# Attention with the key blocks of a step packed into nine full-width blocks of exponentials and a ring of four

## The reference

```python
# first attention: q per head, k and v shared
scores = jnp.einsum('bnhd,bmd->bhnm', q, k) / jnp.sqrt(jnp.float32(D))
scores = jnp.where(causal, -jnp.inf, scores)
out = jnp.einsum('bhnm,bmd->bnhd', jax.nn.softmax(scores, axis=-1), v)
# second attention: k and v per head
scores = jnp.einsum('bhqd,bhkd->bhqk', q, k) / scale + _alibi_bias(H, Tlen)[None]
out = jnp.einsum('bhqk,bhkd->bhqd', jax.nn.softmax(scores, axis=-1), v)
```

## Time and profile before

| | |
|---|---|
| median of three runs | 1051.63 us (1050.88 to 1053.87) |
| the profiled execution, span of its core | 1051.1 us |
| TensorE busy | 997.1 us, 95% of the span |
| VectorE busy | 759.5 us, 72% |
| ScalarE busy | 589.0 us, 56% |
| GpSimd busy | 410.8 us, 39% |
| exponentials (L1403) | 768, 329.0 us |
| values (L1055) | 1536 rows, 163.7 us |
| masks (L760) | 120, 76.2 us |

### The profile page before, as it was taken

One profiled execution on the slowest core, in us unless ns is written; L12 is line 12 of the kernel. 1 busy time (PEld: TensorE's weight loads), 2 busy tenths in 40 slices (PEclk: granted clock), 3 DMA queues, 4 the chain that ended last, 5 costly groups with the idle time before them and its releaser, 6 DMA issues.

```text
span 1051.1 us, 19787 instructions
## 1 busy us (share of the span) xinstructions
PE 997.1 (95%) x6818; PEld 638.7 (61%) x6818; DVE 759.5 (72%) x1564; ACT 589.0 (56%) x1262; POOL 410.8 (39%) x434
## 2 busy tenths in 40 slices
PE   4899999999999999999999999999999999999998
PEld 3533333433348889988886434343343588899887
DVE  6788888888547686447878888888883558764575
ACT  4525776777764335653344657677777643456432
POOL 3420544322443507725743102323234362274470
PEclk9869999999999999999999999999999999999999
DMA  4721212110114415644249533234401152256351
GB/s 133 193 41 30 47 42 43 39 43 13 28 28 149 142 46 155 188 116 118 79 112 227 107 51 57 50 72 74 76 12 44 42 201 60 73 179 165 119 180 51
DMA packets 66755, 95.23 MB, mean 91 GB/s; under 512 B 19669, under 2 KB 50821, under 8 KB 64599
## 3 DMA queue, kind: packets, MB, share of 16 engines
q1 hardware_dynamic: 46645, 52.54, 18.5%
q10 hardware_dynamic: 13100, 22.53, 8.8%
q0 software_dynamic: 6912, 18.88, 7.0%
HBM read 66.59 MB, written 26.67 MB: 89 GB/s over the span
## 4 chain that ended last, share of the span: by engine, by line
PE 74%; DVE 13%; ACT 4%; DMA 3%; issue 3%; POOL 2%; SPq 1%; ACTq 0%; DVEq 0%; POOLq 0%
PE o_ps L1055 14%; PE st_ps L1037 11%; PE su_ps L996 7%; PE st_ps L245 7%; PE st_ps L246 7%; PE st_ps L247 6%; DVE mab L1677 4%; PE st_ps L996 3%; PE o_ps L1195 3%; PE su_ps L1195 3%; PE su_ps L1101 2%; ACT pt L1403 2%; PE st_ps L1230 2%; PE su_ps L1000 2%; DVE xn L1561 1%
## 5 line engine op out<-in xcount | busy, mean ns | idle before, releaser
L1403 ACT ACTIVATE pt<-st_ps 128x512 f32<-128x512 f32 (+3 forms) x768 | 329.0, 495 | 174.4 <-PE st_ps L1037 117.4
L1037 PE MATMUL st_ps<-qs,ks 99*128 99x512 bf16 (+9 forms) x768 | 245.0, 332 | 9.6 <-ACT pt L1403 7.0
L760 POOL TENSOR_SCALAR_AFFINE_SELECT pt<-pt 128x512 f32<-128x512 f32 x120 | 76.2, 635 | 351.5 <-ACT pt L1403 351.5
L1677 DVE TENSOR_REDUCE mab<-su_ps 128x1 f32<-128x512 f32 (+3 forms) x302 | 190.0, 659 | 23.4 <-PE su_ps L1000 16.2
L996 PE MATMUL su_ps<-ks,qs 102*128 102x512 bf16 (+7 forms) x538 | 162.3, 331 | 4.7 <-DVE mc L1677 2.7
L1055 PE MATMUL o_ps<-pt,vp 128*32 128x512 f32 (+3 forms) x1536 | 163.7, 501 | 1.9 <-POOL pt L760 1.0
L1037 PEld LDWEIGHTS st_ps<-qs,ks 99*128 99x128 bf16 (+2 forms) x768 | 73.7, 98 | 116.0 <-ACT pt L1403 65.0
L841 POOL DMA_INDIRECT rows_in<-rows,source x80 | 79.0, 987 | 97.5 <-DVE source L1937 73.7
L1677 DVE TENSOR_REDUCE mab<-st_ps 128x1 f32<-128x512 f32 (+2 forms) x152 | 100.2, 660 | 13.7 <-PE st_ps L1000 10.6
L1429 ACT CAST hh<-hf 128x512 fp32r<-128x512 f32 x64 | 39.7, 621 | 124.4 <-DVE hf L1892 124.4
L996 PEld LDWEIGHTS su_ps<-ks,qs 96*128 96x128 bf16 (+1 forms) x538 | 52.8, 99 | 84.0 <-DVE mab L1677 48.5
(11 more groups left out here) (230 smaller groups left out, 2031.4 us busy)
## 6 DMA issues: line engine op xcount, KB each, us to landing
wu_raw<-w_units_dram SPq DMA_DIRECT2D x32, 384.0 KB, 3.2
outs<-rows_out ACTq DMA_DIRECT2D x40, 256.0 KB, 2.7
q_parts<-hml SPq DMA_DIRECT2D x16, 384.0 KB, 3.4
wexp_raw<-w_units_dram SPq DMA_DIRECT2D x16, 384.0 KB, 7.2
inv<-inverses SPq DMA_DIRECT2D x128, 32.0 KB, 1.8
rows<-xn SPq DMA_DIRECT2D x8, 512.0 KB, 6.6
qs<-q_parts ACTq DMA_DIRECT2D x10, 384.0 KB
k_parts<-hml SPq DMA_DIRECT2D x8, 384.0 KB, 2.5
```

Source lines behind the costliest of these rows:

```text
L760: pool.affine_select(block, block, [[0, 4], [1, P]], ALU.is_ge, 0.0, base=0, channel_multiplier=-1).then_inc(masked, 1)
L1037: last = pe.matmul(bank[KM_BANKS[n % len(KM_BANKS)]][:, lo - CH * part:hi - CH * part], key_stack(l, s)(j)[0:rows, P * kt:P * kt + P], que ...
L1403: act.activation(exponentials(s, q, lo, hi)[:, j, :], bank[KM_BANKS[i % len(KM_BANKS)]][:, lo - CH * part:hi - CH * part], ACT.Exp, scale= ...
L1677: dve.tensor_reduce(to, bank[SU_BANKS[n % len(SU_BANKS)]][:, 0:share * width].rearrange("p (j k) -> p j k", j=share), AX.X, ALU.max).then_ ...
```

## The change

The pairs (`kt`, `part`) of a step are packed into blocks of 512 columns. Six pairs are that wide by themselves; of the other six, (1,0) and (3,0), (2,0) and (6,1), (5,1) and (7,1) lie side by side in one bank. A later step has nine blocks, so 36 pieces (`LATER_BLOCKS`), the first ten, so 40 (`FIRST_BLOCKS`; there (2,0) and (6,1) stay alone, 256 wide, and the first half has three blocks). A joined block has two score matmuls a piece, one exponential, one or two masks, and the values of its two pairs one behind the other. Blocks take the four places of `pt` in turn, and an exponential waits for the values of the block four earlier. In all there are 584 exponentials for 768. GpSimd's other work is bound to masked blocks, of which there are five for eight, and stands at other places; in the last step the two halves' divisions of the step before stand behind the second and third masked block, and the reciprocal roots (`rstds`) together behind the last. `FC_BEHIND`, `PV_LAG` and the lead of the units are as before; the units are spread over the new pieces by the same rule, and `SECOND_AT` of the second layer is 7 for 9.

The diff's core:

```diff
+FIRST_BLOCKS = [((0, 0),), ((1, 0), (3, 0)), ((2, 0),),
+                ((0, 1),), ((1, 1),), ((4, 1),), ((2, 1),), ((5, 1), (7, 1)), ((6, 1),), ((3, 1),)]
+LATER_BLOCKS = [((0, 0),), ((0, 1),), ((1, 0), (3, 0)), ((4, 1),), ((2, 0), (6, 1)), ((1, 1),), ((5, 1), (7, 1)), ((2, 1),), ((3, 1),)]
+HALF_BLOCKS = 3
+FIRST_PIECES = 4 * len(FIRST_BLOCKS)
+RING_OF_BLOCKS = 4
...
-SECOND_AT = (HALF_PIECES - 1, 9)
+SECOND_AT = (HALF_PIECES - 1, 7)
...
+        def exponentials(S, q):
+
+            own, at = divmod((block_base(S) + q) % RING_OF_BLOCKS, 2)
+            return pt[:, own, :, CH * at:CH * at + CH]
...
+                    if masks_after(l, s):
+                        own = exponentials(S, q)
+                        pool.wait_ge(p_ready, piece_base(S) + 4 * q + 4)
+                        for at in diagonals(s, q):
...
+            def last_step(l, i):
+
+                if i == 0:
                     split_unit(l, 0)
-                if kt == 1:
+                if i == 1:
                     divide(l, STEPS - 2, 0)
-                if kt == 2:
+                if i == 2:
+                    divide(l, STEPS - 2, 1)
+                if i == 3:
                     split_unit(l, 1)
-                if kt == 3:
-                    divide(l, STEPS - 2, 1)
-                    rstds(2 * l + 1, 0, 1)
-                if kt == 4:
-                    rstds(2 * l + 1, 1, 2)
+                if i == 4:
+                    rstds(2 * l + 1, 0, 2)
...
+                for kt, part, lo, hi, at in spans(s, q):
+                    diagonal = lo == P * kt and not masks_after(l, s)
+                    last = pe.matmul(out_b[:, at:at + hi - lo], key_stack(l, s)(j)[0:rows, P * kt:P * kt + P],
+                                     query_columns(s, slice(0, rows), j, lo, hi), start=True, stop=not diagonal)
...
+                for i, (kt, part, lo, hi, at) in enumerate(spans(s, q)):
+                    if kt == 0:
+                        wait(pe, ou_done, 2 * S - 1 + part)
+                    for j in range(4):
...
-                        if last_quad(S, q) is not None:
-                            act.wait_ge(pv_done, last_quad(S, q) + 1)
-                        act.activation(exponentials(s, q, lo, hi)[:, j, :], bank[KM_BANKS[i % len(KM_BANKS)]][:, lo - CH * part:hi - CH * part], ACT.Exp,
+                        wait(act, pv_done, block_base(S) + q - RING_OF_BLOCKS + 1)
+                        act.activation(exponentials(S, q)[:, j, 0:width_of(s, q)], bank[KM_BANKS[i % len(KM_BANKS)]][:, 0:width_of(s, q)], ACT.Exp,
```

More of the change, by code:

```diff
@@ L142, in units_behind_pieces @@
 def units_behind_pieces(l, lead):
-    work = np.array([[queries(s, n // 4)[1] - queries(s, n // 4)[0] + P for n in range(PIECES)] for s in range(STEPS)], float)
-    at = (np.arange(STEPS)[:, None] + np.cumsum(work, 1) / work.sum(1)[:, None]).flatten()
+    work = [np.array([width_of(s, n // 4) + P for n in range(4 * len(blocks(s)))], float) for s in range(STEPS)]
+    at = np.concatenate([s + np.cumsum(w) / w.sum() for s, w in enumerate(work)])
     cost = np.array([share * width + P for _, _, _, share, width, _ in SU] + [4 * CH], float)
@@ L163, in units_behind_pieces @@
         for u, t in enumerate(s - 1 - lead + through):
-            while at[n] < t - 1e-9 or u > 1 and n < PIECES - 1:
+            while at[n] < t - 1e-9 or u > 1 and n < FIRST_PIECES - 1:
                 n += 1
@@ L1046, in values @@
                 b, g = divmod(s, G)
-                kt, part = quads(s)[q]
-                if kt == 0:
-                    wait(pe, ou_done, 2 * S - 1 + part)
-                lo, hi = queries(s, q)
-                if lo == P * kt and masks_after(l, s):
-                    pe.wait_ge(masked, QT * mask_turn(l, s) + kt + 1)
-                pe.wait_ge(p_ready, PIECES * S + 4 * q + 4)
-                for j in range(4):
-                    last = pe.matmul(o_ps[32 * j:32 * j + 32, lo:hi], vp[:, QT * b + kt, 4 * g + j if l else 4 * (g % 2), :],
-                                     exponentials(s, q, lo, hi)[:, j, :], start=kt == 0,
-                                     stop=kt == (QT if part else HALF) - 1)
+                if diagonals(s, q) and masks_after(l, s):
+                    pe.wait_ge(masked, QT * mask_turn(l, s) + sum(len(diagonals(s, n)) for n in range(q + 1)))
+                pe.wait_ge(p_ready, piece_base(S) + 4 * q + 4)
+                for i, (kt, part, lo, hi, at) in enumerate(spans(s, q)):
+                    if kt == 0:
+                        wait(pe, ou_done, 2 * S - 1 + part)
+                    for j in range(4):
+                        last = pe.matmul(o_ps[32 * j:32 * j + 32, lo:hi], vp[:, QT * b + kt, 4 * g + j if l else 4 * (g % 2), :],
+                                         exponentials(S, q)[:, j, at:at + hi - lo], start=kt == 0, stop=(q, i) == last_of(s, part))
                 last.then_inc(pv_done, 1)
@@ L1084, in attention @@
                             transpose_half(l, 1)
-                    if s == STEPS - 1 and piece in FC_BEHIND:
-                        output_projection(l, FC_BEHIND[piece])
-                for q in range(NQ - PV_LAG, NQ):
+                    if s == STEPS - 1 and 4 * q + j in FC_BEHIND:
+                        output_projection(l, FC_BEHIND[4 * q + j])
+                for q in range(len(LATER_BLOCKS) - PV_LAG, len(LATER_BLOCKS)):
                     values(l, STEPS - 1, q)
```

128 lines of the change are left out of this document (57 added, 71 removed).

## The result

The changed kernel takes 1043.54 us (median of four runs, 1042.43 to 1046.84); the kernel before took 1051.26 beside it (the three runs given ahead and one more, 1050.33 to 1053.87). The ratio is 0.9923, with a 95% interval of 0.9901 to 0.9945. 1044.8 had been forecast. The profiled execution, 1046.84 us with a span of 1045.1, is the slowest of the four, so the two spans differ by 6.0 where the medians differ by 7.7.

What follows compares the result with a forecast made beforehand. TensorE's work and waits were taken as the bound. 10.0+2.0-2.6-2.0-.6 = 6.8 us less than the median of 1051.63 gave 1044.8; forecast 1038.5 to 1048.5 (chance .60), 8-in-10 range 1037.5 to 1056.

Steps and rivals of the forecast that it cites:

- What bounds the kernel: TensorE, busy 997.1 of 1051.1 us: time can be won only where it works or waits for something.
- Joined blocks: In a later attention step, three value groups fewer on TensorE save .6 us (ends .45 and .75).
- both terms of a join: A group's fixed .15 us and the .1 for entering it from a score matmul; with both, a later step saves .75.
- the back-to-back row: Trace row of adjacent 256- and 128-column value groups at half clock: .72 us at full clock against .93 alone, saving .21.
- The first rival: Joins save nothing or waits return: a step gains .3 to .5 instead of 1.0; 1049 to 1054 us, chance .19.
- Waits: TensorE's 1.32 us of waits a steady step become .65 to 1.2; with joins, the step gains 1.0, ten steps 10.0.
- The maxima: Their chain lands 4.9 to 6.1 us behind the transposition, within the distance of 6.2; seventh steps gain 2.0 over two layers.
- The second rival: Splitting waits for both division halves, so maxima land 7.5 us behind the transposition in every step: 1055 to 1060, chance .14.
- The last step: Later output projections delay VectorE's serial row and the next projection, 34.5 us behind the step's start: loss 2.6 (1.0 to 4.0).
- The clock: TensorE idles in the last steps' tails and may drop to half clock behind them: loss 2.0 us (0 to 5).
- the opening's 6.8: In the first layer's opening, TensorE ran 6.8 us at half clock after being busy 1.57 of 3.80; cost 3.4.
- First steps: Both layers' first steps: a longer group closing a half costs .64, two joins return .4; loss .6 (gain 2 to loss 3).

Runs made afterwards that it cites:

- with the loads: Changed kernel with the last step's reciprocals early and the third and fourth units' weight loads ahead of the last spreading of inverses: 1031.97 us, ratio 0.9790.
- the second combination: Changed kernel with last step's reciprocals early, third and fourth units' weight loads ahead of the last spreading of inverses, last step's units .05 step earlier: 1031.47, ratio 0.9785.

## Why the prediction was right, by its steps

*What bounds the kernel.* Right: the gains and losses that were traced are all in what TensorE does or waits for.

*Joined blocks, .6 a step.* The work fell by .72 to .74: both terms of a join are saved, the upper end. The .2 taken for a join from the back-to-back row at half clock was a little low. The first rival, that a join saves nothing, is right to this extent: of the .72 only .21 reach the step, since the rest returns as the transposition's wait.

*Waits, 1.32 to .65-1.2.* Right: .83. The transposition waits .50 (.47 had been said), the units' banks .27, and the units behind the splitting nothing. (The pair of scores at 223.43 that the prediction calls 128 wide is one of 128 and the next step's first of 512 columns; its .28 of columns and its wait are right.) The step of 28.51 is at the lower end of 28.5 to 29.0, and the value taken, a gain of 1.0, was too small by .24; over the third to sixth steps 1.7. Another .9 is the fourth step of the first layer, 30.68 before and 28.51 now, whose extra length had been left out of the sum. Before, a group of values there (169.89) stood .9 waiting for a mask at 169.15, which came behind GpSimd's splitting of weights (3.45 from 165.75); with GpSimd's work at other places TensorE has no such wait there.

*The maxima.* The distance of 6.17 had been counted right, the landing came at the low end, 5.0 of 4.9 to 6.1. What was wrong is the other end: that a splitting of 2.95 would still fit. The later transposition showed such a splitting (2.9), and the step took .83 more, because VectorE's lateness reaches TensorE through the units' banks before it reaches it through the landing. The second rival was nearer than I had thought: .17 us separate the changed kernel from a step that loses, and this needs the wait for one half of the division, not for both. The Trainium skill's page "SBUF — State Buffer", section "Who interferes with whom", says that an instruction blocked on the shared pair of ports waits for the whole of the other one. The trace of the later transposition agrees: the division's first half ran from 213.93 to 215.20, the third part, started at 214.07, ended at 215.34.

*The last step.* Right in place and size: projections 34.84 and 33.82 for 34.5; loss 1.4 and .7 a layer, 2.2 for 2.2 without the weights. That the reciprocals stand behind the normalisation while their sums lie ready was in the rows, and in the sum only as .55 of slack. It was the cheapest thing to mend.

*The clock.* The term that was mis-sized in the tail: 2.4 and 2.9 at the projections, of which some 5 show in the tails, for 2.0 taken of 0 to 5. A drop had been put at half the length of the opening's 6.8, and one and a bit of them were taken; there is one behind each tail, and they lie over 4.6 and 5.5 us of work, of which half, 2.3 and 2.7, is lost.

*First steps.* First and second step together won .8 and 1.4 for a forecast of .7 each; the seventh .9 and 1.3 for 1.0. In three of the other kernels with the same first steps (the reciprocals early, with the loads, and the second combination) the second layer's pair took 66.8 where it took 68.4 here: in this execution TensorE was granted .50 there from 618.50 to 621.90, in those 1.00 throughout.

## What to carry to other kernels

Cheaper work ahead of a wait is partly given back: before counting a saving on the bound engine, look at what the next handover behind it waits for, and whether that wait has the room. Where a change moves work within a step, the instructions that were tied to its pieces (projections, reciprocals, loads) move against it too. What became late here was an instruction that lay ready behind others in a queue, and moving that one line gave about as much again as the change (.9832 for .9923). And a ring for buffers should be tried without the regrouping that came with it: alone it was worth as much here, by the ratios (.9912 for .9923).

## What the runs showed of the hardware

A delay of .17 us became 1.26 us on VectorE, because its cast and its subtraction of two SBUF operands then met GpSimd's mask and division (.63 for .21, 1.27 for .60), and with GpSimd's division elsewhere the subtraction took .28; beside a cast of weights on GpSimd it took 1.44. After 4.3 us without a matmul TensorE ran the next 4.6 us at half clock; 60 small matmuls of 3.5 us in that idle time kept it at full clock. Shorter waits went either way: behind one of 1.9 us it ran at half clock up to 197.00, behind one of 2.2 it did not (maxima sent late, 193.94 and 226.36). A second group of values in the same four column groups costs nothing to enter behind another (1.01 for two halves, 1.00 for one whole), while each separate group costs .24.
